# An attention and mixture-of-experts kernel: tile lists through a one-hot product, y copied a tile later, gather ahead of add

## What is computed

```python
x = x + xattn(layernorm(x), ctx)      # 16 batches x 56 tokens x 512; 1500 context rows each
# ffn, on t = 896 tokens, 16 experts, the 4 best of each token:
scores = sigmoid(x @ gate_w.T) + bias
topk_w, topk_idx = top_k(scores, 4)
topk_w = topk_w / (sum(topk_w) + 1e-20)
cw  = sum(one_hot(topk_idx, 16) * topk_w[..., None], axis=1)
z   = silu(x @ Wg[e].T) * (x @ Wu[e].T)          # per expert e, inner size 256
out = sum_e (z * cw[:, e]) @ Wd[e].T
out = out + silu(x @ Sg.T) * (x @ Su.T) @ Sd.T   # the shared expert
x   = x + out
```

## Time and profile before

| | us |
|---|---|
| median of three runs | 545.14 |
| lowest, highest | 544.95, 545.25 |
| profiled execution, whole | 546.24 |
| its span (first to last instruction of the trace) | 544.5 |

### The profile page before, as it was taken

One profiled execution on the slowest core, in us unless ns is written; L12 is line 12 of the kernel. 1 busy time (PEld: TensorE's weight loads), 2 busy tenths in 40 slices (PEclk: granted clock), 3 DMA queues, 4 the chain that ended last, 5 costly groups with the idle time before them and its releaser, 6 DMA issues.

```text
span 544.5 us, 10804 instructions
## 1 busy us (share of the span) xinstructions
PE 481.4 (88%) x2472; PEld 291.5 (54%) x2473; DVE 260.0 (48%) x707; ACT 155.8 (29%) x303; POOL 119.3 (22%) x100
## 2 busy tenths in 40 slices
PE   4999999999999999998789869779998898899960
PEld 1565354453636363543358636567776666676740
DVE  3223345462737354352537864625565466555420
ACT  0001321020202020210213253435455456444430
POOL 1000000000000000000002233335554465335531
PEclk9989999999999999999899979979999899899985
DMA  9999999999999999999646676785858687445452
GB/s 212 393 419 427 398 424 415 409 427 396 424 402 426 403 422 404 422 426 415 258 127 174 150 202 191 235 254 94 221 100 265 137 207 210 78 88 98 98 64 32
DMA packets 28231, 149.04 MB, mean 274 GB/s; under 512 B 4072, under 2 KB 4200, under 8 KB 16424
## 3 DMA queue, kind: packets, MB, share of 16 engines
q1 hardware_dynamic: 15832, 123.08, 57.1%
q0 software_dynamic: 8720, 20.21, 20.5%
q10 hardware_dynamic: 3664, 5.57, 3.3%
HBM read 133.84 MB, written 15.01 MB: 273 GB/s over the span
## 4 chain that ended last, share of the span: by engine, by line
PE 49%; DMA 33%; issue 7%; DVE 3%; ACT 2%; POOLq 1%; ACTq 1%; POOL 1%; DVEq 1%; SPq 0%
DMA ctx_cols<-in_ctx_t 15%; PE b L680 13%; PE scores L550 11%; PE b L574 8%; DMA taken<-h_rows,take_at 8%; DMA out<-y_sb,add_at 5%; PE b L538 4%; PE b L500 4%; PE scores L512 2%; PE scores L680 2%; PE b L564 1%; DMA w_qk<-in_wk 1%; DMA out<-y_sb,shared_at 1%; DMA h_rows<-h 1%; POOL out L459 1%
## 5 line engine op out<-in xcount | busy, mean ns | idle before, releaser
L550 PE MATMUL scores<-ctx_cols,g_t 128*64 128x500 f32 x384 | 85.2, 586 | 2.6 <-DMA ctx_cols<-in_ctx_t 2.5
L574 PE MATMUL b<-ctx_rows,probs_t 125*64 125x512 f32 (+1 forms) x384 | 86.0, 598 | 0.0
L459 POOL DMA_INDIRECT out<-y_sb,add_at x34 | 54.5, 1604 | 89.0 <-ACT add_at L931 46.8
L423 POOL TENSOR_TENSOR rstd<-var_eps,neg_half 128x1 f32<-128x1 f32 x16 | 8.8, 549 | 268.4 <-DVE var_eps L1022 268.4
L680 PE MATMUL b<-w_hi,taken_hi 128*128 x136 | 56.2, 414 | 1.1 <-ACT taken_hi L908 1.1
L680 PE MATMUL b<-w_lo,taken_hi 128*128 x136 | 54.8, 403 | 0.0
L1280 DVE TENSOR_TENSOR w_lo<-w_raw,w_hi (+1 forms) x33 | 39.7, 1223 | 30.2 <-ACT w_hi L897 26.6
L550 PEld LDWEIGHTS scores<-ctx_cols,g_t 128*64 128x64 f32 x384 | 26.1, 136 | 51.8 <-issue 46.0
L574 PEld LDWEIGHTS b<-ctx_rows,probs_t 125*64 125x64 f32 (+1 forms) x384 | 26.3, 137 | 48.0 <-issue 47.1
L444 POOL DMA_INDIRECT taken<-h_rows,take_at x34 | 42.7, 1257 | 28.4 <-DVE take_at L1306 20.2
L897 ACT CAST w_hi<-w_raw (+1 forms) x33 | 33.8, 1047 | 29.0 <-PE b L680 9.1
(11 more groups left out here) (213 smaller groups left out, 677.2 us busy)
## 6 DMA issues: line engine op xcount, KB each, us to landing
ctx_rows<-in_ctx SPq DMA_DIRECT2D x48, 1024.0 KB, 19.5
ctx_cols<-in_ctx_t SPq DMA_DIRECT2D x32, 1500.0 KB, 22.8
w_raw<-in_experts SPq DMA_DIRECT2D x11, 1536.0 KB, 7.5
h_rows<-h ACTq DMA_DIRECT2D x16, 115.5 KB
taken<-h_rows SPq DMA_DIRECT2D x7, 264.0 KB, 3.1
out<-xs ACTq DMA_DIRECT2D x2, 784.0 KB
shared_raw<-in_shared SPq DMA_DIRECT2D x1, 1536.0 KB, 32.4
xs<-in_x ACTq DMA_DIRECT2D x12, 112.0 KB
```

Of the source, the lines that this page charges most:

```text
L459: nc.gpsimd.indirect_dma_start(out[:, :], bass.IndirectOffsetOnAxis(ap=add_at[i][:, 0:1], axis=0), y_sb[:, i * DIM:(i + 1) * DIM], None, c ...
L550: last = nc.tensor.matmul(scores[HALF * b:HALF * (b + 1), n, 0:CHUNK], g_t[:, k, HALF * b:HALF * (b + 1)], ctx_cols[:, at:at + CHUNK], sta ...
L574: last = nc.tensor.matmul(b3[HALF * b:HALF * (b + 1), :], probs_t[0:rows_in(p), at:at + HALF], ctx_rows[0:rows_in(p), g, b, c * DIM:(c + 1 ...
```

## The change

- The 34 tiles' lists are brought into tile order once. `list_rows` stops at `place_at`. PE transposes it (`lay_places`), ScalarE keeps the transpose (`keep_places`), PE multiplies it with a one-hot matrix `tile_picks` (column of tile j has a one where its list is; `pick_tiles`), and VectorE makes `tile_at` and `tile_to`, 52 columns each, from the product (`tile_rows`). `T_COL` and `T_EXPERT` leave `plan`; the one-hot matrix and a row of expert numbers come from two broadcast products and `keep_picks`.
- `name_take` copies column t-7 of `tile_at`; `take_weight` compares the expert number with 0 to 15, multiplies with the 16 weights and sums, and stands with `name_take` ahead of `silu_rows`. It waits for the gather and for the row products of the tile two before.
- y of routed tiles goes to three banks by turns (the three of `scores`), and `keep_y(t-3)` takes the place of `keep_y(t-2)`; `down(t)` in the loop waits for the copy of tile t-3.
- GpSimd copies the add's column itself, within `add`, in place of ScalarE's `name_add`; its round is `gather(t+5)`, then `add(t)`, and the gather waits for the transpose that frees its buffer.

```diff
@@ helpers
+        def y_bank(eng, t):
+            if isinstance(t, int) and t < SHARED:
+                return (b3[:, :], scores[:, 1, :])[t % 2]
+            at = (t + 1) % Y_BANKS * 512
+            ...
+            return y_ring[:, bass.ds(at, 512)]
@@ gpsimd
             def add_shared(t):
+                pool.wait_ge(added[t % 2], t // 2 * 16 + 16)
                 pool.wait_ge(ysb_ready, t + 1)
             def gather(t, i):
                 pool.wait_ge(take_named, t - (SHARED - 1))
                 settle(pool)
+                pool.wait_ge(tt_ready, t - 1)
+                settle(pool)
             def add(t, i):
                 first = entry(pool, T_FIRST, t - SHARED, TILES + SHARED)
-                pool.wait_ge(added[0], pool.snap((first + 1) // 2 * 16 + 16, min_val=16, max_val=16 * TILES))
+                pool.wait_ge(added[i], t // 2 * 16 + 16)
                 settle(pool)
-                pool.wait_ge(added[1], pool.snap(first // 2 * 16 + 16, min_val=16, max_val=16 * TILES))
-                settle(pool)
-                pool.wait_ge(add_named, t - (SHARED - 2))
+                nc.gpsimd.tensor_copy(add_at[i][:], tile_to[:, bass.ds(t - SHARED, 1)]).then_inc(add_named, 1)
+                others = first // 2 if i == 0 else (first + 1) // 2
+                pool.wait_ge(added[1 - i], pool.snap(others * 16 + 16, min_val=16, max_val=16 * TILES))
                 settle(pool)
                 pool.wait_ge(ysb_ready, t + 1)
+                settle(pool)
+                pool.wait_ge(add_named, t + 1)
                 settle(pool)
             add_shared(6)
+            pool.wait_ge(tiles_named, 1)
             with pool.Fori(0, n_inner - 1) as pair:
                 for k in range(2):
                     t = pair * 2 + (SHARED + k)
+                    gather(t + 5, k)
                     add(t, 1 - k)
-                    gather(t + 5, k)
             t = n_inner * 2 + (SHARED - 2)
-            add(t, 1)
             gather(t + 5, 0)
-            for k in range(1, 6):
+            for k in range(6):
                 add(t + k, 1 - k % 2)
@@ tensor
+                for at, column in ((C_PICK, place_col), (C_EXPERT, expert_t)):
+                    last = nc.tensor.matmul(scores[:, 0, at:at + AHEAD], column[:].to_broadcast([P, P]),
+                                            ident[:, 0:AHEAD], start=True, stop=True)
+                last.then_inc(picks_ready, 1)
+            def lay_places():
+                pe.wait_ge(plan_ready, 1)
+                pe.wait_ge(places_ready, 1)
+                nc.tensor.transpose(scores[:, 2, 0:P], place_at[:], ident).then_inc(places_laid, 1)
+            def pick_tiles():
+                pe.wait_ge(places_kept, 1)
+                nc.tensor.matmul(scores[:, 2, P:P + AHEAD], place_t[:], tile_picks[:], start=True, stop=True
+                                 ).then_inc(tiles_picked, 1)
@@ down
-                if not isinstance(t, int) or t > 1:
+                if not isinstance(t, int):
+                    pe.wait_ge(ysb_ready, t - 2)
+                    settle(pe)
+                elif t > 1:
                     pe.wait_ge(ysb_ready, t - 1)
-                    settle(pe)
+                bank = y_bank(pe, t)
@@ tensor, shared tiles
             shared_transpose(6)
+            lay_places()
             down(4, 0, shared_hi, shared_lo, 0)
+            pick_tiles()
             up_hi(6, 0, shared_hi, shared_lo, 0)
@@ scalar
             taken_to_hi(6)
+            keep_places()
             keep_y(3, 1)
             ...
-                keep_y(t - 2, i)
-                if not isinstance(t, int):
-                    name_add(t - 2, i)
+                if not isinstance(t, int) or t > SHARED:
+                    keep_y(t - 3, 1 - i)
                 more_thirds(t + 1)
             ...
             half(t, 0)
+            keep_y(t - 3, 1)
             keep_y(t - 2, 0)
-            name_add(t - 2, 0)
             keep_y(t - 1, 1)
-            name_add(t - 1, 1)
             z_to_hi(t)
             keep_y(t, 0)
-            name_add(t, 0)
@@ vector
+            def tile_rows():
+                dve.wait_ge(tiles_picked, 1)
+                places = scores[:, 2, P:P + AHEAD]
+                ch.mark(nc.vector.tensor_copy(tile_at[:], places))
+                ...
+                nc.vector.scalar_tensor_tensor(tile_to[:], places, -float(PAIR_TOKENS), wrapped[:], ALU.add, ALU.add
+                                               ).then_inc(tiles_named, 1)
             def take_weight(t, i):
-                e = entry(dve, T_EXPERT, t - SHARED, EXPERTS - 1)
-                nc.vector.tensor_copy(taken_w[:, i:i + 1], taken[i][:, bass.ds(e + DIM, 1)]).then_inc(w_ready, 1)
+                dve.wait_ge(gathered[i], (t - SHARED) // 2 * 16 + 16)
+                settle(dve)
+                dve.wait_ge(z_rows_ready, t - 1)
+                settle(dve)
+                nc.vector.scalar_tensor_tensor(picked_w[:, i * EXPERTS:(i + 1) * EXPERTS], iota16, expert_row[:, bass.ds(t - SHARED, 1)],
+                                               taken[i][:, DIM:ROW], ALU.is_equal, ALU.mult, accum_out=taken_w[:, i:i + 1]
+                                               ).then_inc(w_ready, 1)
+            keep_picks()
             shared_silu(4)
             ...
             list_rows()
-            dve.wait_ge(plan_ready, 1)
-            name_take(SHARED, 1)
             shared_silu(5)
             taken_to_lo(6)
+            tile_rows()
+            dve.wait_ge(dve_step, ch.now())
+            name_take(SHARED, 1)
             name_take(SHARED + 1, 0)
             ...
             def step(t, i):
                 z_to_lo(t - 1)
+                take_weight(t + 1, 1 - i)
+                name_take(t + 3, 1 - i)
                 silu_rows(t, i)
                 taken_to_lo(t + 1)
-                take_weight(t + 1, 1 - i)
-                name_take(t + 3, 1 - i)
                 more_thirds(t + 1)
```

More of the change, by code:

```diff
@@ L36 @@
 TILES = 48
-TABLES = 8
+TABLES = 6
 SHARED = TOKENS // P
-T_TURNS, T_COL, T_EXPERT, T_PIECES, T_TURN, T_FIRST, T_LOAD, T_HALF = (i * TILES for i in range(TABLES))
+Y_BANKS = 3
+AHEAD = TILES + 4
+T_TURNS, T_PIECES, T_TURN, T_FIRST, T_LOAD, T_HALF = (i * TILES for i in range(TABLES))
 C_ID, C_TRI, C_IOTA, C_REGION = 0, P, 2 * P, 2 * P + EXPERTS
@@ L718, in down @@
                 for k in range(KI):
-                    last = part(y_banks[i], zt_lo, hi, at + UP, k, DIM, stop=(k == KI - 1))
+                    last = part(bank, zt_lo, hi, at + UP, k, DIM, stop=(k == KI - 1))
                 last.then_inc(yt_ready, 1)
@@ L1154, in _ @@
             nc.vector.tensor_copy(shared_at[:], shared_place[:]).then_inc(shared_named, 1)
-            for rows in (list_at, list_to):
-                ch.mark(nc.vector.tensor_scalar(rows[:, LISTS:], dump_row[:].to_broadcast([P, EXPERTS]), -float(P), None,
-                                                ALU.add))
+            ch.mark(nc.vector.tensor_scalar(place_at[:, LISTS:], dump_row[:].to_broadcast([P, EXPERTS]), -float(P), None,
+                                            ALU.add))
             wide = [P, PAIRS, TILES_MAX]
```

82 lines of the change are left out of this document (46 added, 36 removed).

## The result

| | before | after |
|---|---|---|
| median of 18 executions each (us) | 545.55 | 551.01 |
| lowest, highest | 542.94, 553.28, and one of 957.74 | 547.54, 557.15 |
| profiled execution (us) | 546.24 | 548.49 |
| its span (us) | 544.5 | 546.2 |

The ratio after to before is 1.0092, 95% interval 1.0064 to 1.012. The forecast was 542.8 with a range of 536.5 to 548.8; the median lies 2.2 us above the range, and the sign is wrong.

What follows compares the result with a forecast made beforehand. PE steps of 5.2 us bound the expert half, with 15 us of gather waits. Terms -3.4 - 0.8 - 1.6 + 3.5 = -2.3 us gave a 543.9 profiled execution, 542.8 median; 8-in-10 range 536.5 to 548.8.

Steps and rivals of the forecast that it cites:

- What bounds the kernel: Expert half: PE steps of 5.2 us are ideal; 25 us loose, 15 of them waits for gathered tiles.
- who makes a gather late: GpSimd's queue: gather leaves 5.0 us after the transpose two tiles before; late when landing takes over 5.3 us.
- Part 1: Steady-state loop: gather ahead of add and y copied a tile later cancel; dropping name_add leaves -0.8 us.
- Part 2: Loop entry, tiles 7 to 16: gather(12) no longer behind add(7), stall shrinks; -3.4 us, start's 1.2 included.
- case C: Rival at tile 12: stall moves on, gathers 13 and 14 land as slowly as gather 12; 544.9 us, chance 0.20.
- Part 3: Start, up to tile 7: relay over three engines for lists in tile order names tile 7 later; +1.2 us.
- Part 4: VectorE naming and weights: register loads leave, so splitting in weight bursts starts sooner; -1.6 us.
- Part 5: Tail after tile 40: one more add outstanding, add(37) waits for its later y copy; +3.5 us.
- Part 6: Index copy on GpSimd: taken at 0 because GpSimd has room; the copy itself priced at 0.5 us.
- case D: Rival: index copy makes GpSimd the bound in rounds stretched by VectorE splits; +6, 548.8 us, chance 0.15.
- the difference carries over: From profiled execution to median: the profiled execution's 1.1 us above the median stays, turning 543.9 into 542.8.
- the rest on the slow side: Remaining outcomes, chance 0.08: a start or tail dearer than bounded, mostly slower.

Runs made afterwards that it cites:

- the lists alone: Changed kernel with y copied two tiles behind and the add ahead of the gather, both as in the kernel before: 541.5 us, ratio 0.9846 to before.
- the late copy alone: Changed kernel with add(t) put back ahead of gather(t+5), y still copied three tiles behind: 648.63 us, ratio 1.1939 to before.
- its second run: The changed kernel measured once more, unchanged, on the chip of the first experiments: 551.47 us, ratio 1.0053 to before.
- the early copy: Changed kernel with y copied two tiles behind again (keep_y(t-2)), gather still ahead of add: 539.09 us, ratio 0.98; on another chip 537.92 us, ratio 0.9909.
- the swap alone: Kernel before with gather(t+5) put ahead of add(t) in GpSimd's round, nothing else changed: 555.9 us, ratio 1.0101 to before.

## Why the prediction was wrong, by its own steps

**What bounds the kernel, who makes a gather late.** Right for the gathers: their count behind an add explains where they leave in every run. It does not explain the gain of the lists alone.

**Part 1, the two edits cancel (-0.8).** Right in mechanism: lags of 4.65 to 4.7 us where "about 4.8" was forecast, and the run with the late copy alone shows its weight, and that of the swap that takes it back, at a whole tile. The size between tiles 14 and 29 was -0.1. The waits of tile 24 (2.06) and of tile 22 (2.59, the longest behind tile 12 in `before`) are gone, but tile 18 got one of 2.11. Gathers b+6 late in place of b+5, as I had said: tiles 13, 14 and 18 stand six behind 7, 8 and 12.

**Part 2, the entry (-3.4 with the start).** This is the step that failed. By tile 14 the profiled execution was 0.79 us behind `before`, not 3.4 ahead. Tile 12 came at 352.68 (352.8 forecast). Tile 13 came at 361.02 for 359.3, and tile 14 at 369.02 for 365. The working let gathers land late but gave the adds in front of them the 5.5 us of the one landing that `before` showed at this place; the landing was 8.46 (the add itself started at 343.44 for 343.0), and the wait went through tile 7's and tile 8's adds to gathers 13 and 14. The term that was mis-sized is this landing, 5.5 taken and 8.46 measured, and with it the wait of tile 7's add and those behind it. It is case C, by the landing of an add rather than of a gather, and 2.1 us later than its 366.9. The trace of `before` had gathers of 3.5 to 8.0 us beside the same loads; an add's landing should have had the same bounds. In the three full profiles of kernels with the late copy behind the new lists (`after`, its second run, and the one with ScalarE's copy) tiles 7 to 14 take 45.71, 44.91 and 44.85 us; in `before` 47.25, and 51.94 in the profile of an execution of 552.88 us, which can't stand for the usual one. Against 47.25 the part brings 1.5 to 2.4 us, in all three well short of the 4.6.

**Part 3, the start (+1.2).** Mis-sized: +2.33, of which the relay is 1.0 and a longer landing the rest. Tile 7 came at 322.11 to 324.12 in all profiles with the new lists but one (319.75), and at 318.69 to 322.92 in five with the old ones, so the landing can hide the relay's 1.0 or double it. The naming of tile 7 was forecast within 0.5 us.

**Part 4, VectorE (-1.6).** Right in sign, low in size: the bursts from tile 29 to 32 took 18.57 us for 21.73. This is the difference that repeats best: 18.57 to 19.14 in eight profiles with the new lists (the ninth is the late copy without the swap, where every step is long), 20.00 to 22.10 in five with the old.

**Part 5, the tail (+3.5).** Right: +3.72, and 14.4 to 15.0 us in the kernels with the early copy.

**Part 6 and case D.** The copy measured 0.18 to 0.21 us in most rounds, 0.66 to 0.77 at times, taken at 0.5, and costs nothing, since it lies ahead of the wait for y. The Trainium skill ("SBUF — State Buffer", section "Who interferes with whom") says that a VectorE operation with two SBUF inputs contends with a GpSimd operation that reads SBUF. The traces agree. Two of the long copies in `after` begin while a split runs and end 0.04 us behind it or less; one of the two, with its split:

```profile
345.70 1.23 DVE L1332 TENSOR_TENSOR w_lo<-w_raw,w_hi  x1 [0.93 <-ACT w_hi L943]
346.31 0.66 POOL L475 COPY add_at<-tile_to 128x1 int32 x1
```

And in `before`, of 34 gathers 14 begin while a split runs and take 1.01 to 1.93 us to make (13 of them over 1.2), the other 20 take 1.02 at most. The four other long copies (0.75 to 0.77 us) stand in the tail, each beginning a microsecond into the making of an add (519.22 in an add from 518.20 on) with no split beside it; what lengthens those stays open. So a GpSimd operation can be held up beside a split, as case D had it, and its price was never paid, because the copy has room. The run with the copy on ScalarE confirms that.

**From one execution to the median.** The step "the difference carries over" failed as much as part 2 did, if in another way. Of the 5.9 us between the medians 545.14 and 551.01, 2.25 are between the two profiled executions and 3.6 come from where these lie among their like (1.1 above, 2.5 below). A forecast of 543.9 for a profiled execution that took 548.49 is off by 4.6; the forecast of the median by 8.2. The range was built from bounds within one execution, with no term for how landings vary between executions. Why `after` sits higher in its spread than its profile suggests stays open: the runs have one profile each, and the fastest execution of `after` (547.54) is near the profiled one.

**The chances.** Cases C and D and the rest on the slow side had 0.43 together, spread over 544.9 to 548.8; the 0.23 given to a slower kernel is D and the rest alone, so C's upper end was counted at nothing. The tail's cost is in every profile with the late copy (+3.7 or more), and the relay's in every one with the new lists (gather 7 leaves at 314.94 to 315.71 in nine, at 313.86 to 314.73 in five with the old); the gain of the entry hung on landings. That asymmetry should have moved the forecast.

## What to carry to other kernels

When two edits shift the same queue in opposite directions, count each in whole steps and ask whether one of them is needed at all: here the lists with the early name bring most of the gain (ratio 0.985), the swap with the early copy at most a little more (0.98 and 0.99 in two measurements), and the late copy gives the lead back and adds a tail that nothing hides. A reordering on a queue can gain only when the name or data of what moves ahead is early too; otherwise what stands behind it waits, as the adds did in the swap alone. Bound every landing beside large loads by the longest seen there for its kind or a like one, adds as well as gathers, and carry the executions' own spread into the range.

## What the runs showed of the hardware

**TensorE's granted clock can drop around a wait for a gather, and the step behind it is then slow.** The clock in stretches of `before` around tile 12's wait (columns: stretch, its length, busy us of PE, PEld, DVE, ACT, POOL, granted clock, DMA share, GB/s):

```profile
351.00:357.00 6.00, 0.79 (x4) 0.41 (x3) 2.36 (x4) 0.38 (x1) 2.84 (x2) 0.74 0.92 280
357.00:360.00 3.00, 3.00 (x10) 2.49 (x9) 0.84 (x2) 1.23 (x3) 0.00 (x0) 0.50 0.75 203
360.00:363.00 3.00, 3.00 (x14) 2.41 (x13) 0.15 (x1) 0.32 (x1) 2.58 (x2) 0.89 0.81 258
363.00:368.00 5.00, 5.00 (x27) 3.99 (x25) 2.22 (x6) 3.13 (x7) 1.56 (x1) 1.00 0.86 266
```

PE, idle for most of six microseconds, runs the three behind them at 0.50, which is the lower of its two levels (1.2 of 2.4 GHz), busy throughout, and is back at 1.00 by 363. In `after` it was at 0.75 behind tile 18's wait of 2.11 us:

```profile
395.00:399.00 4.00, 4.00 (x16) 3.15 (x15) 1.28 (x2) 1.42 (x2) 3.28 (x3) 0.75 0.55 82
```

The step behind this wait took 6.8 us where 5.0 to 5.3 are usual, so a wait of 2.11 cost some 3.7 with what followed. I had seen the slow step at tile 13 of `before` and not that new waits can bring their own. Not every wait does. These are two more stretches of `before`, the first behind tile 22's wait of 2.59 us, the second behind tile 24's of 2.06:

```profile
415.00:418.00 3.00, 3.00 (x16) 2.40 (x14) 0.79 (x3) 0.42 (x2) 1.65 (x2) 1.00 0.46 125
426.00:429.00 3.00, 3.00 (x10) 2.48 (x9) 0.84 (x2) 1.22 (x3) 0.00 (x0) 0.51 0.32 90
```

The longer wait was followed by full clock and a step of 5.18 us, the shorter by 0.51 and one of 6.38. What decides it these runs don't tell, so 1.2 to 1.7 us for the step behind a wait is a price that may or may not come.

**Landings of like transfers vary by half and more beside loads, and between executions.** The gather of tile 7 landed in 5.70 to 8.18 us in two executions each of `before` and `after`; the last shared add in 5.51 and 8.82 in two of `before`, in 8.46 in `after`, and in 4.61 in `before` with the loads cut down. With the loads cut down, the waits for gathers in `before` fell from 15.2 to 2.7 us, with gathers and adds unchanged in size and number; 3.1 of these 12.5 us are tile 7's, whose gather lands before the first of the cut loads starts.
